# Routed experts by blocks of 128 slots in place of pairs of blocks, in an attention and mixture-of-experts kernel

## The chip, the core and the metric

The kernel runs on one core of a Trainium2 chip. A core has five engines that run their own instruction streams and meet only at semaphores: TensorE (PE), VectorE (DVE), ScalarE (ACT), GpSimd (POOL) and SyncE (SP). SP, ACT and POOL also issue DMA transfers between the chip's memory (HBM) and the on-chip memory. Matrix products land in PSUM, which has eight banks of 128 partitions by 512 fp32 values. The metric is the device time of one execution in microseconds, lower is better; what is shown before is the median of three timed runs and one profiled execution.

## What is computed

`x` has 4 sequences of 256 tokens with 256 channels. The first half of the kernel adds cross attention to it; the second half adds a feed-forward layer with two of eight routed experts per token and a shared expert. The part that matters here:

```python
    scores = xf @ gate_w.T                       # 1024 tokens, 8 experts
    ew, ei = jax.lax.top_k(scores, TOP_K)        # the two best
    ew = jax.nn.softmax(ew, axis=-1)
    x1 = jax.nn.silu(jnp.einsum('td,ehd->teh', xf, w_gate))
    x3 = jnp.einsum('td,ehd->teh', xf, w_up)
    expert_out = jnp.einsum('teh,edh->ted', x1 * x3, w_down)
    comb = jnp.einsum('ta,tae->te', ew, onehot)
    routed = jnp.einsum('te,ted->td', comb, expert_out)
    shared = jax.nn.silu(xf @ sh_gate.T) * (xf @ sh_up.T) @ sh_down.T
    sgate = jax.nn.sigmoid(xf @ se_gate_w.T)
    return (routed + sgate * shared).reshape(Bb, Tt, Cc)
```

`xf` is the layer norm of `x` behind the attention, and the whole is added to `x`. An expert has 128 hidden units, the shared one 256. Everything is fp32.

## The kernel before

**The routing by slots.** The kernel doesn't compute all experts for all tokens. Each token's normalised row, with its number and its lower expert's number behind it, is written twice to a list in HBM (`slots_dram`), in the region of each of its two experts: 16 indirect DMAs of GpSimd. The 2048 entries are then worked through in blocks of 128 rows, each of one expert. As each expert's last block may be part empty, there are at most 16 + 7 = 23 blocks (`BLOCKS`). VectorE works out a table with the first row (`row_of`) and the expert (`expert_of`) of each block. SP, PE and DVE each load what they need of it into registers (line 285, `TENSOR_LOAD`), since the addresses of row loads (SP), of down weights (PE) and of hidden weights (DVE) depend on it.

**One block.** SP loads its rows to `xg` (132 KB, six buffers, line 314). PE transposes them into PSUM (`gather_T`, line 1048), ACT copies the transpose to `xgT` (line 506). DVE copies the expert's gate and up weights to `hidden_w` (`stage`, line 798, four buffers). PE forms gate and up (`routed_hidden`, line 1064), ACT takes SiLU of the gate (`r_silu`, line 514), DVE multiplies by up (`r_act`, line 806), PE forms the down product (`routed_down`, line 1079), ACT copies it to `y_sb` (lines 522 and 526), and GpSimd scatters the 128 result rows to `routed_dram` (`send_y`, line 365) by places that DVE works out from the rows' tails (`places`, lines 776 and 780).

**By pairs.** Blocks go through this in pairs `p` of two (12 pairs, the last of one block). One PSUM bank holds the transposes of a pair, one its gate and up, one its two results. Each of `xgT`, `r_silu` and `r_act` has two buffers of a pair, `y_sb` has three (`NY`). All hand-overs are once a pair, except that from pair `SINGLE` = 9 on the results are copied and released block by block. PE's order in the loop is hidden(p), transposes of pair p + 2, down(p - 1). ACT's is SiLU(p), copy of the transposes of p + 2, copy of the results of p - 1. DVE's is `r_act`(p), weights of p + 2, places of p + 2. GpSimd only sends.

**Around the loop.** The order is written out by hand. The shared expert runs in two halves of 512 tokens and two units of 128 hidden values (`shared_gate`, `shared_up`, line 998; `shared_act`, line 759; `shared_down`, line 1034). Before the loop PE does gate(1,0), gate(1,1), up(1,0) and the first part of up(1,1); DVE does the residual of half 0 (`base(0)`, line 768), the product `shared_act(1, 0)`, the register load (`experts`), and weights and places of two pairs. The second part of up(1,1) and its product lie in the first turn of the loop. PE's first transposes wait for `shared_act(1, 0)`, as they take over its PSUM bank, and its first hidden products for both SiLUs of half 1. Behind the loop PE does `shared_down(1, ...)` and DVE `base(1)`. When all sends but the last have landed, SP and ACT load the lower half of the results (`lower_y`), and after the last the upper one (`upper_y`); DVE adds both with the tokens' shares (lines 811 and 817), and the output is stored.

## Time and profile before

| | before |
|---|---|
| three timed runs | 105.22, 107.85, 108.12 us, median 107.85 |
| profiled execution | 105.32 us, of which the span is 103.5 |
| PE busy | 85.5 us (83%) |
| DVE busy | 62.1 us (60%) |
| ACT busy | 46.5 us (45%) |
| POOL busy | 44.8 us (43%) |
| 23 sends of results | 23.6 us, mean 1025 ns |
| hidden products (line 1064) | 22.6 us, idle before them 1.1 |
| down products (line 1079) | 12.0 us, idle before them 0.3 |

The span is the time from the first to the last instruction of the profiled execution. Busy time counts the engines' own work, not semaphore waits or the issue of DMAs. Matmuls overlap in the array, so their durations can't be added up; a chain or the distance between starts tells what one costs. The trace puts every instruction at its time from the span's start; idle time before an instruction is given in brackets with what ended it.

### The profile page before, as it was taken

What the parts mean: (1) busy time and instruction counts of PE and PEld (TensorE: products, weight loads), DVE (VectorE), ACT (ScalarE), POOL (GpSimd) and SP (SyncE); (2) the same over time, 40 slices, a digit from 0 to 9 for tenths busy, and PEclk for the clock granted to TensorE, in tenths of its full rate; (3) what the DMA queues carried; (4) which work ended last, traced back from release to release, by engine and by line L of the source; (5) the groups of instructions that cost most, each with busy time, mean ns of one, the idle gap of its engine ahead of it and who ended that gap; (6) DMA issues with size and microseconds to landing.
All of it is one profiled execution on the core that took longest, in us unless ns stands there. A gap on an engine that the chain in (4) does not pass through costs nothing.

```text
span 103.5 us, 1864 instructions
## 1 busy us (share of the span) xinstructions
PE 85.5 (83%) x514; PEld 68.5 (66%) x514; DVE 62.1 (60%) x274; ACT 46.5 (45%) x104; POOL 44.8 (43%) x60
## 2 busy tenths in 40 slices
PE   6799999997999999996799999999999989600000
PEld 2386789895974478443789999999999968400000
DVE  1188989999999889202986444566444320604990
ACT  0556657758685991433036454466454361000000
POOL 7012002388676777300000567668667677710000
PEclk9999999999999999999999999999999999985555
DMA  2975999992232222256163434655412212059946
GB/s 20 376 267 133 410 413 401 333 348 77 93 108 104 104 104 104 104 142 177 26 186 104 112 107 134 188 152 161 154 46 100 96 56 101 0 90 355 369 180 225
DMA packets 10586, 17.50 MB, mean 169 GB/s; under 512 B 1613, under 2 KB 6095, under 8 KB 10576
## 3 DMA queue, kind: packets, MB, share of 16 engines
q1 hardware_dynamic: 7264, 10.63, 32.7%
q0 software_dynamic: 1872, 4.27, 11.2%
q10 hardware_dynamic: 1440, 2.49, 6.6%
q8 instruction: 4, 0.07, 0.3%
q14 instruction: 6, 0.05, 0.1%
HBM read 10.85 MB, written 7.44 MB: 177 GB/s over the span
## 4 chain that ended last, share of the span: by engine, by line
PE 64%; DMA 12%; DVE 12%; issue 3%; DVEq 3%; POOLq 1%; POOL 1%; ACT 1%; ACTq 0%
PE bank L1064 20%; PE bank L998 12%; PE bank L1079 9%; DMA upper_y<-routed_dram 6%; PE bank L1048 4%; DMA proj_sb<-proj 4%; PE bank L942 4%; PE bank L1034 4%; PE bank L898 3%; PE bank L923 3%; DVEq L285 2%; DMA routed_dram<-y_sb,place 2%; PE bank L906 2%; DVE x L642 2%; PE bank L907 2%
## 5 line engine op out<-in xcount | busy, mean ns | idle before, releaser
L365 POOL DMA_INDIRECT routed_dram<-y_sb,place x23 | 23.6, 1025 | 25.0 <-DVE place L780 15.4
L1064 PEld LDWEIGHTS bank<-xgT,hidden_w 128*128 128x128 f32 x184 | 22.4, 192 | 2.3 <-issue 1.8
L1064 PE MATMUL bank<-xgT,hidden_w 128*128 128x128 f32 x184 | 22.6, 275 | 1.1 <-DVE hidden_w L798 1.1
L352 POOL DMA_INDIRECT slots_dram<-rows,slot x16 | 15.7, 981 | 6.8 <-issue 4.4
L998 PE MATMUL bank<-xnT,ffn_sb 128*128 128x512 f32 (+1 forms) x36 | 14.6, 550 | 0.0
L806 DVE TENSOR_TENSOR r_act<-bank,r_silu 128x256 f32<-128x256 f32 (+1 forms) x12 | 5.0, 414 | 15.9 <-ACT r_silu L514 14.2
L1079 PE MATMUL bank<-ffn_sb,r_act 128*128 x46 | 12.0, 382 | 0.3 <-ACT y_sb L526 0.3
L514 ACT ACTIVATE r_silu<-bank 128x256 f32<-128x256 f32 (+1 forms) x12 | 4.5, 376 | 15.3 <-PE bank L1064 15.3
L998 PEld LDWEIGHTS bank<-xnT,ffn_sb 128*128 128x128 f32 x36 | 6.6, 190 | 5.5 <-issue 5.3
L798 DVE COPY hidden_w<-ffn_sb 128x512 f32 x23 | 8.7, 419 | 1.9 <-issue 1.9
L1079 PEld LDWEIGHTS bank<-ffn_sb,r_act 128*128 128x128 f32 x46 | 7.8, 190 | 1.2 <-issue 0.7
L506 ACT COPY xgT<-bank 128x512 f32<-128x512 f32 (+1 forms) x12 | 6.8, 568 | 3.5 <-PE bank L1048 3.0
L942 PE MATMUL bank<-mix,xT 128*128 128x276 f32 x32 | 8.2, 401 | 0.0
L1048 PE MATMUL bank<-ident,xg 128*128 128x128 f32 x46 | 7.1, 275 | 0.3 <-DMA xg<-slots_dram 0.3
L1034 PE MATMUL bank<-ffn_sb,sh_act 128*128 128x256 f32 x32 | 7.3, 382 | 0.0
L942 PEld LDWEIGHTS bank<-mix,xT 128*128 128x128 f32 x32 | 5.9, 190 | 1.3
L522 ACT COPY y_sb<-bank 128x512 f32<-128x512 f32 x9 | 5.3, 586 | 3.3 <-PE bank L1079 3.3
L1034 PEld LDWEIGHTS bank<-ffn_sb,sh_act 128*128 128x128 f32 x32 | 6.0, 190 | 1.0 <-DVE sh_act L759 0.2
L1048 PEld LDWEIGHTS bank<-ident,xg 128*128 128x128 f32 x46 | 5.3, 141 | 1.4 <-DVE sh_act L759 0.8
L768 DVE SCALAR_TENSOR_TENSOR x<-bank,sgate,x 128x256 f32<-128x256 f32 x8 | 3.5, 480 | 3.9 <-PE bank L1034 3.8
L811 DVE SCALAR_TENSOR_TENSOR x<-lower_y,share_lower,x 128x256 f32<-128x256 f32 x8 | 3.3, 478 | 4.2 <-DMA lower_y<-routed_dram 4.2
L344 POOL TENSOR_TENSOR rstd<-veps,neg_half 128x2 f32<-128x2 f32 x2 | 1.4, 715 | 9.1 <-DVE veps L607 9.1
(119 smaller groups left out, 128.9 us busy)
## 6 DMA issues: line engine op xcount, KB each, us to landing
ffn_sb<-ffn SPq DMA_DIRECT2D x2, 1536.0 KB, 9.6
xg<-slots_dram SPq DMA_DIRECT2D x23, 132.0 KB, 2.2
slots_dram<-empty SPq DMA_DIRECT2D x1, 1056.0 KB, 14.2
x_sb<-x ACTq DMA_DIRECT2D x4, 256.0 KB, 5.0
ffn_sb<-ffn SPq DMA_DIRECT2D x1, 768.0 KB, 4.3
lower_y<-routed_dram SPq DMA_DIRECT2D x2, 256.0 KB, 4.2
lower_y<-routed_dram ACTq DMA_DIRECT2D x2, 256.0 KB, 4.5
upper_y<-routed_dram SPq DMA_DIRECT2D x2, 256.0 KB, 5.6
```

The lines of the kernel that those rows point to most:

```text
L352: pool.indirect_dma_start(out=slots_dram[:, :], out_offset=bass.IndirectOffsetOnAxis(ap=slot[:, i, a:a + 1], axis=0), in_=rows[:, i, :], i ...
L365: pool.indirect_dma_start(out=routed_dram[0:planes * TOKENS, :], out_offset=bass.IndirectOffsetOnAxis(ap=place[:, j:j + 1], axis=0), in_=y ...
L506: act.copy(xgT[:, p % 2, :, 0:n, :], XG_BANK[p % 2][:, :].rearrange("p (k b n) -> p k b n", k=KT, b=2)[:, :, 0:n, :]).then_inc(xgT_stored, 1)
L522: act.copy(y_sb[:, p % NY, :, :], tiles(Y_BANK[p % 2])).then_inc(y_stored, 2)
L798: dve.tensor_copy(hidden_w[:, j % NW, :], ffn_sb[:, u, 0:2 * L].rearrange("p o n -> p (o n)")).then_inc(staged, 1)
L806: dve.tensor_tensor(r_act[:, p % 2, 0:n, :], hidden_of(p, 1), r_silu[:, p % 2, 0:n, :], ALU.mult).then_inc(r_act_ready, 1)
L942: last = pe.matmul(ps[:, 0:L + 2 * R], xT[:, b, k, t * P:(t + 1) * P], mix[:, b % 2, k, :], start=(k == 0), stop=(k == KT - 1))
L998: last = pe.matmul(ps[:, c0:c1], ffn_sb[:, E + u, c:c + P], xnT[:, k, h * N + c0:h * N + c1], start=(k == 0), stop=(k == KT - 1))
L1034: last = pe.matmul(tiles(SH_OUT[h][t // 2])[:, t % 2, :], sh_act[:, h, u, t * P:(t + 1) * P], ffn_sb[:, E + u, 2 * L:3 * L], start=(u == 0 ...
L1048: last = pe.transpose(ps[:, k, b, :], xg[:, j % NXG, k * P:(k + 1) * P], ident[:])
L1064: last = pe.matmul(hidden_of(p, kind)[:, j % 2, :], hidden_w[:, j % NW, c:c + P], xgT[:, p % 2, k, j % 2, :], start=(k == 0), stop=(k == K ...
L1079: last = pe.matmul(y_of(j), r_act[:, p % 2, j % 2, :], ffn_sb[:, u, 2 * L:3 * L].rearrange("p o n -> p (o n)"), start=True, stop=True)
```

## The change

The routed stage goes by blocks. PSUM banks, buffers and hand-overs are those of one block; a result has a buffer of its own among six, and is sent with a wait of its own. Gate and up, and the results, use other banks than before, so that the loop's first products wait for no bank of the shared expert. Places of a block are worked out in its own turn, and the weights three blocks ahead. VectorE loads its registers before `shared_act(1, 0)`, and TensorE forms up(1,0) before gate(1,1).

```diff
-PAIRS = (BLOCKS + 1) // 2
-JB = 2 * PAIRS
+JB = BLOCKS + 1
-NY = 3
+NY = 6
-        xgT = sb("xgT", [P, 2, KT, 2, P])
-        r_silu = sb("r_silu", [P, 2, 2, P])
-        r_act = sb("r_act", [P, 2, 2, P])
+        xgT = sb("xgT", [P, 2, KT, P])
+        r_silu = sb("r_silu", [P, 2, P])
+        r_act = sb("r_act", [P, 2, P])
-        y_sb = sb("y_sb", [P, NY, 2, L])
+        y_sb = sb("y_sb", [P, NY, L])
-        SH_OUT = [[bank[6], bank[3]], [bank[7], bank[2]]]
+        SH_OUT = [[bank[6], bank[3]], [bank[1], bank[3]]]
-        GU_BANK = [bank[1], bank[2]]
-        Y_BANK = [bank[6], bank[3]]
+        GU_BANK = [bank[4], bank[5]]
+        Y_BANK = [bank[6], bank[2]]
...
 SP, loads of rows
                 if j >= NXG:
-                    sp.wait_ge(xgT_ready, (j - NXG) // 2 + 1)
-                    sp.wait_ge(place_ready, (j - NXG) // 2 + 1)
+                    sp.wait_ge(xgT_ready, j - NXG + 1)
+                    sp.wait_ge(place_ready, j - NXG + 1)
...
 POOL, send_y
-                p, k = j // 2, j % 2
-                if p >= SINGLE:
-                    pool.wait_ge(y_stored, j + 1)
-                elif k == 0:
-                    pool.wait_ge(y_stored, 2 * p + 2)
-                if k == 0:
-                    pool.wait_ge(place_ready, p + 1)
+                pool.wait_ge(y_stored, j + 1)
+                pool.wait_ge(place_ready, j + 1)
...
 ACT
+            def store_xgT(j):
+                act.wait_ge(xgT_ready, j + 1)
+                if j >= 2:
+                    act.wait_ge(gu_ready, j - 1)
+                act.copy(xgT[:, j % 2], XG_BANK[j % 2][:, 0:KT * P].rearrange(
+                    "p (k n) -> p k n", k=KT)).then_inc(xgT_stored, 1)
...
+            def store_y(j):
+                act.wait_ge(y_ready, j + 1)
+                if j >= NY:
+                    act.wait_ge(y_sent[j % NY], 16 * (j // NY))
+                act.copy(y_sb[:, j % NY, :], y_of(j)).then_inc(y_stored, 1)
...
+            for j in range(BLOCKS):
+                routed_silu(j)
+                if j + 2 < BLOCKS:
+                    store_xgT(j + 2)
+                if j >= 1:
+                    store_y(j - 1)
+            store_y(BLOCKS - 1)
...
 DVE
+            def places(j):
+                dve.wait_ge(xg_in[j % NXG], 16 * (j // NXG + 1))
+                then(dve.tensor_scalar(plane[:, j:j + 1], xg[:, j % NXG, L + 1:L + 2], expert[:, j:j + 1],
+                                       float(TOKENS), ALU.is_equal, ALU.mult))
+                dve.tensor_tensor(place[:, j:j + 1], plane[:, j:j + 1], xg[:, j % NXG, L:L + 1].bitcast(I32),
+                                  ALU.add).then_inc(place_ready, 1)
...
+            def routed_act(j):
+                dve.wait_ge(r_silu_ready, j + 1)
+                if j >= 2:
+                    dve.wait_ge(y_ready, j - 1)
+                dve.tensor_tensor(r_act[:, j % 2, :], hidden_of(j, 1), r_silu[:, j % 2, :],
                                   ALU.mult).then_inc(r_act_ready, 1)
...
             base(0)
-            shared_act(1, 0)
             experts()
             stage(0)
-            places(0)
             stage(1)
-            places(1)
+            shared_act(1, 0)
+            stage(2)
             routed_shares()
-            for p in range(PAIRS):
-                routed_act(p)
-                if p + 2 < PAIRS:
-                    stage(p + 2)
-                    places(p + 2)
-                if p == 0:
+            for j in range(BLOCKS):
+                routed_act(j)
+                if j + 3 < BLOCKS:
+                    stage(j + 3)
+                if j == 0:
                     shared_act(1, 1)
+                places(j)
...
 PE
+            def routed_hidden(j):
+                if j >= 2:
+                    pe.wait_ge(r_act_ready, j - 1)
+                pe.wait_ge(xgT_stored, j + 1)
+                pe.wait_ge(staged, j + 1)
...
+            def routed_down(j):
+                if j < 2:
+                    pe.wait_ge(base_ready, 1)
                 else:
+                    pe.wait_ge(y_stored, j - 1)
+                pe.wait_ge(r_act_ready, j + 1)
...
             shared_gate(1, 0)
+            shared_up(1, 0)
             shared_gate(1, 1)
-            shared_up(1, 0)
...
+            for j in range(BLOCKS):
+                routed_hidden(j)
+                if j + 2 < BLOCKS:
+                    gather_T(j + 2)
+                if j == 0:
                     shared_up(1, 1, [1])
                 else:
+                    routed_down(j - 1)
+            routed_down(BLOCKS - 1)
```

VectorE's order between the residual of half 0 and its first `r_act`, before (`L285` is the register load, the `ISA` rows set an address from a register, `L759` is the shared product):

```order
L768 SCALAR_TENSOR_TENSOR x<-bank,sgate,x 128x256 x4
L759 TENSOR_TENSOR sh_act<-bank,sh_silu 128x512
L285 TENSOR_LOAD expert_of
L798 ISA
L798 COPY hidden_w<-ffn_sb 128x512
L798 ISA
L798 COPY hidden_w<-ffn_sb 128x512
```

and with the change (its line numbers are 27 to 33 lower there: `L741`, `L732`, `L271`, `L766`):

```order
L741 SCALAR_TENSOR_TENSOR x<-bank,sgate,x 128x256 x4
L271 TENSOR_LOAD expert_of
L766 ISA
L766 COPY hidden_w<-ffn_sb 128x512
L766 ISA
L766 COPY hidden_w<-ffn_sb 128x512
L732 TENSOR_TENSOR sh_act<-bank,sh_silu 128x512
L766 ISA
L766 COPY hidden_w<-ffn_sb 128x512
```

The load and two copies of weights now stand ahead of the shared product, a third behind it, and no places are worked out here.

TensorE's order at the loop's entry, before (`L998` is shared gate or up, `L1048` transposes of rows, `L1064` hidden products, `L1079` a down product with its address):

```order
L998 MATMUL bank<-xnT,ffn_sb 128x512
L1048 MATMUL bank<-ident,xg 128x128 x8
L1064 MATMUL bank<-xgT,hidden_w 128x128 x8
L1048 MATMUL bank<-ident,xg 128x128 x4
L998 MATMUL bank<-xnT,ffn_sb 128x512
L1064 MATMUL bank<-xgT,hidden_w 128x128 x8
L1048 MATMUL bank<-ident,xg 128x128 x4
L1079 ISA
L1079 MATMUL bank<-ffn_sb,r_act 128x256
L1079 ISA
L1079 MATMUL bank<-ffn_sb,r_act 128x256
```

and with the change:

```order
L964 MATMUL bank<-xnT,ffn_sb 128x512
L1011 MATMUL bank<-ident,xg 128x128 x4
L1024 MATMUL bank<-xgT,hidden_w 128x128 x4
L1011 MATMUL bank<-ident,xg 128x128 x2
L964 MATMUL bank<-xnT,ffn_sb 128x512
L1024 MATMUL bank<-xgT,hidden_w 128x128 x4
L1011 MATMUL bank<-ident,xg 128x128 x2
L1035 ISA
L1035 MATMUL bank<-ffn_sb,r_act 128x256
L1024 MATMUL bank<-xgT,hidden_w 128x128 x4
L1011 MATMUL bank<-ident,xg 128x128 x2
```

Two blocks are transposed ahead of the first hidden product in place of four, and each step is half as long; the number of matmuls is the same.

## Rows read from the trace of the kernel before

**Rows 1.** Busy time by stretch: PE, PEld, DVE, ACT, POOL, then clock.
```profile
49.85:86.13 36.28, 35.99 (x271) 33.98 (x272) 18.59 (x84) 16.81 (x35) 19.68 (x20) 1.00 0.38 116
```

**Rows 2.** Chain of waits at the loop's entry: start, duration, what.
```profile
46.42 0.05 issue
46.47 2.32 DVEq L285
...
49.85 2.02 PE bank L1064 x16
```

**Rows 3.** Order of time ahead of the loop, all engines: start, duration, idle before.
```profile
40.18 1.81 DVE L768 SCALAR_TENSOR_TENSOR x<-bank,sgate,x 128x256 f32<-128x256 f32 x4
...
40.91 6.17 PE L998 MATMUL bank<-xnT,ffn_sb 128*128 128x512 f32 x14
...
46.33 0.69 DVE L759 TENSOR_TENSOR sh_act<-bank,sh_silu 128x512 f32<-128x512 f32 x1 [4.34 <-PE bank L998]
...
47.08 0.87 PE L1048 MATMUL bank<-ident,xg 128*128 128x128 f32 x6
...
48.28 0.44 PE L1048 MATMUL bank<-ident,xg 128*128 128x128 f32 x2 [0.33 <-DMA xg<-slots_dram]
```

**Rows 4.** Order of time on ACT, single shapes near the loop's end.
```profile
79.96 0.37 ACT L506 COPY xgT<-bank 128x256 f32<-128x256 f32 x1
...
82.55 0.38 ACT L514 ACTIVATE r_silu<-bank 128x256 f32<-128x256 f32 x1 [1.12 <-PE bank L1064]
...
84.31 0.28 ACT L514 ACTIVATE r_silu<-bank 128x128 f32<-128x128 f32 x1 [0.52 <-PE bank L1064]
```

**Rows 5.** Order of time on DVE, single shapes near the loop's end.
```profile
80.44 0.42 DVE L798 COPY hidden_w<-ffn_sb 128x512 f32 x1
80.77 0.21 DVE L776 TENSOR_SCALAR plane<-xg,expert 128x1 f32<-128x1 f32 x1
81.01 0.16 DVE L780 TENSOR_TENSOR place<-plane,xg 128x1 int32<-128x1 f32 x1
...
84.62 0.29 DVE L806 TENSOR_TENSOR r_act<-bank,r_silu 128x128 f32<-128x128 f32 x1 [1.23 <-ACT r_silu L514]
```

**Rows 6.** Chain of waits, one pair of the steady loop.
```profile
59.34 1.78 PE bank L1064 x16
61.12 0.44 PE bank L1048 x4
61.56 0.87 PE bank L1079 x4
```

**Rows 7.** Chain of waits at the loop's exit.
```profile
84.27 0.45 PE bank L1079 x2
...
85.18 0.24 issue
85.42 0.71 PE bank L1079 x2
...
86.21 0.38 ACT y_sb L526
...
89.94 2.12 DMA routed_dram<-y_sb,place
```

**Rows 8.** Loads of rows (line 314): time from issue to landing.
```profile
DMA to landing us min/median/max: 1.9/2.2/3.4
```

**Rows 9.** Order of time on ACT and POOL: a copy of results, and sends.
```profile
80.84 0.59 ACT L522 COPY y_sb<-bank 128x512 f32<-128x512 f32 x1 [0.51 <-PE bank L1079]
...
60.79 0.98 POOL L365 DMA_INDIRECT routed_dram<-y_sb,place  x1 [0.68 <-issue]
...
80.62 1.09 POOL L365 DMA_INDIRECT routed_dram<-y_sb,place  x1 [0.30 <-issue]
82.20 0.98 POOL L365 DMA_INDIRECT routed_dram<-y_sb,place  x1 [0.48 <-issue]
```

**Rows 10.** Order of time on DVE behind the loop: the first adds of results.
```profile
94.66 3.26 DVE L811 SCALAR_TENSOR_TENSOR x<-lower_y,share_lower,x 128x256 f32<-128x256 f32 x8 [4.18 <-DMA lower_y<-routed_dram]
```

More of the change, by code:

```diff
@@ L263, in wait_for_lower @@
             for i in range(NY):
-                mine = [j for j in range(LAST) if j // 2 % NY == i]
+                mine = [j for j in range(LAST) if j % NY == i]
                 queue.wait_ge(y_sent[i], 16 * len(mine))
         def wait_for_upper(queue):
-            queue.wait_ge(y_sent[LAST // 2 % NY], 16 * rows_sent(LAST // 2 % NY))
+            queue.wait_ge(y_sent[LAST % NY], 16 * rows_sent(LAST % NY))
         def load_lower(queue, k):
@@ L770, in base @@
                 last.then_inc(base_ready, 1)
-            def places(p):
-                for j in range(2 * p, 2 * p + blocks_in(p)):
-                    dve.wait_ge(xg_in[j % NXG], 16 * (j // NXG + 1))
-                    last = dve.tensor_scalar(plane[:, j:j + 1], xg[:, j % NXG, L + 1:L + 2], expert[:, j:j + 1],
-                                             float(TOKENS), ALU.is_equal, ALU.mult)
-                then(last)
-                for j in range(2 * p, 2 * p + blocks_in(p)):
-                    last = dve.tensor_tensor(place[:, j:j + 1], plane[:, j:j + 1],
-                                             xg[:, j % NXG, L:L + 1].bitcast(I32), ALU.add)
-                last.then_inc(place_ready, 1)
+            def places(j):
[4 more added lines that the diff above has]
+                                  ALU.add).then_inc(place_ready, 1)
             on_chip = []
```

137 lines of the change are left out of this document (32 added, 105 removed).

## The prediction

> **What bounds the kernel now.** I read three views in turn: busy time by stretch, the chain of waits, the order of time on each engine. In the routed stage TensorE does 35.99 us of work in 36.28 us at granted clock 1.00 [rows 1]: while the stage runs, it is the bound. VectorE (18.59), ScalarE (16.81) and GpSimd (19.68) each have about half their time over, so what they gain or lose in total is worth nothing; only when they hand something over counts.
>
> The chain of waits shows two places where TensorE isn't the bound. The first is the entry. VectorE takes the shared product at 46.33, then its register load of 2.32 us, and only then copies the first weights; TensorE's first hidden product starts at 49.85 [rows 2]. VectorE had stood idle for 4.34 us before that product, since its part of the residual ended at 40.18 + 1.81 = 41.99 [rows 3]. TensorE, done with shared work at 47.08, transposed four blocks and then waited [rows 3]. The second place is the exit. TensorE's last down product ends at 86.13 and its copy at 86.59, but the last send starts at 89.94 and lands 2.12 us later [rows 7]. Since results are released by pairs, GpSimd starts late: the first pair is copied long after its first block was done, and the last seven sends, from 82.20 [rows 9] to 89.94, follow each other at 7.74/6 = 1.29 us, a queue that TensorE has left behind.
>
> **Entry.** The register load moves into the idle stretch: 41.99 + 2.32 = 44.3, and two weight copies at 0.42 [rows 5] end by 45.3 with their issue. The second shared up product now comes before the second gate product. From 40.91 eight passes at 6.17/14 = 0.44 us give gate and up of unit 0 [rows 3], so up ends at 44.4 where it ended at about 46.2; the shared product (0.69, [rows 3]) runs 45.3 to 46.0 and is there before TensorE wants its buffers at 47.08. The second gate product, 1.7 us later, feeds a SiLU that ScalarE fits into its own idle time, and whose product is wanted only inside the loop. So at 47.08 TensorE starts as before, but transposes two blocks ahead in place of four. One block takes 0.44 alone [rows 3], its copy 0.37 [rows 4], with about 0.2 for two hand-overs: hidden product 0 starts at 48.1, not 49.85: **minus 1.75 us**. Ends of the unknown: nothing won, if the loads of rows are late (blocks 0 to 2 were there by then, since their transposes ran through, and only the fourth was waited for, 0.33 us [rows 3]); or 1.9 if the hand-overs overlap.
>
> **Steady loop.** Per pair TensorE spends 1.78 + 0.44 + 0.87 = 3.09 us with no gap between [rows 6]; per block the same instructions take 1.54. They are not more, only interleaved finer. What changes is the notice that each wait gets. Say hidden product j ends at t. SiLU of one block takes 0.28 [rows 4], the product 0.29 [rows 5], hand-overs 0.1: r_act is ready at t + 0.7. TensorE comes to down product j after 0.22 + 0.43 + 0.89 + 0.22 = 1.76 us: 1.06 us to spare (it was 2.6). ScalarE per block: 0.28 + 0.37 + 0.37 = 1.02 [rows 4] of 1.54. VectorE: 0.29 + 0.42 + 0.21 + 0.16 = 1.08 [rows 5]. All fit, so I cost the split at zero for both; their cover is TensorE, and without it the extra would be one fixed part per instruction, 2 x 1.02 against 0.38 [rows 4] + 0.59 + 0.59 [rows 9] = 1.56 per pair on ScalarE, 0.48 us. The transposes of two more blocks now lie inside the loop: 2 x 0.22 = **plus 0.44 us**. The load of row block j + 6 now waits for the places of block j, which follow its r_act: issued at t + 1.6, landed after 2.2, at most 3.4 us [rows 8], so at t + 5.0 at worst; TensorE wants it at four periods, t + 6.2. The cover is 1.2 us; the load was issued a pair and more earlier before. TensorE's waits double (one set per block). I bound that by nothing and by 0.05 us a block, 1.1 us in all, which is the size of the bare step behind a wait in the chain [rows 2]; I take 0, since all of them are satisfied in advance and its rows stand gapless across pair boundaries.
>
> **Exit.** Call H the end of the last hidden product: it was 84.27, with down product 21 ending 0.45 later [rows 7]. Now H = 84.27 - 1.75 + 0.44 = 82.96. Down product 21 ends at 83.41, its copy at 83.86. A send starts 0.77 us after its copy: the copy that ends at 80.84 + 0.59 = 81.43 has its send at 82.20 [rows 9]. Send 21 starts at 84.63. Send 20 came 1.3 us before, as the period without a transpose is 1.32, so there is no queue. Down product 22 no longer waits for a copy, only for r_act 22 (H + 0.65, then 0.24 to start, 0.71 to run [rows 7]): it ends at 84.55, and its send could start at 85.8; 1.29 after send 21 it does, at 85.92. Before, 89.94: **minus 4.0 us**. Of this the last 2.7 are the queue that is gone, the rest is the entry less the two transposes.
> Behind the last send nothing changes: the lower half of the results is loaded when send 21 has landed, the upper when send 22 has, the adds begin at 94.66 after 4.18 us of waiting for the load [rows 10]. The residual of the second half ended before that wait, at 90.5; it moves ahead with TensorE by about 1.6, to 88.9, and the load's landing by 4.0, to 90.7, so it stays hidden. Two more semaphores are waited for at the queues, under 0.1.
>
> **Sum.** The profiled execution took 105.32 us (span 103.5): minus 4.0 gives 101.3 (span 99.5). The three timed runs read 105.22, 107.85 and 108.12, so two of four executions are 2.6 us above the others, and the one trace shows nothing of why. Their mean with the profiled one is 106.6; minus 4.0 is 102.6, which I forecast, between 101.3 and 103.9 for the two groups.
>
> **Rivals.**
> *A. GpSimd's turn per send becomes the bound (slower).* Before, every second send of a pair had no wait of its own and started 0.30 after its predecessor; now each waits for its own copy. If the 0.77 us between copy and send can't overlap the send before, a turn is 0.99 to 1.11 plus 0.77, about 1.83. The first send starts at 52.9 (down product 0 ends at 51.7: 48.1 + 0.89 + 0.22 + 0.86 + 0.89 + 0.22 + 0.43, and 1.2 for copy and send), the last at 52.9 + 22 x 1.83 = 93.2, 3.2 after today's: 108.5 on the profiled execution's scale, 109.8 on the forecast's. It decides from a turn of (89.94 - 52.9)/22 = 1.68 on. For it: the idle before the first send of a pair, 0.68 [rows 9]. Against: the copy that ended at 81.43 did so while a send ran until 81.71, and the next started at 82.20, 0.49 after it, not 0.77 [rows 9]. With 0.49 a turn is 1.48 to 1.60 and would cost at most 22 x 0.06 = 1.3, less as soon as a queue forms and the gap falls to 0.30.
>
> *B. VectorE's weight copies hold up the sends.* A second send of a pair, which runs beside such copies, took 1.09, a first one without them 0.98 [rows 9]. Before, two copies lay together and touched every second send; now one lies under each. At the measured 0.11 a turn is 1.40, still under 1.54, and the sum stands. If instead each send had to stand through a whole copy, a turn were 0.98 + 0.42 + 0.30 = 1.70: last send at 52.9 + 22 x 1.70 = 90.3, no gain, 107.0 on the forecast's scale. The Trainium skill (SBUF — State Buffer, the section "SBUF: two separate sides") says that an fp32 copy within SBUF on VectorE takes the port that GpSimd needs to write descriptors, and that the later one blocks fully. By that rule this rival would be the case, and the sum would be near zero; the trace's 0.11 speaks against its full size.
>
> *C. Finer grain leaves gaps on TensorE.* 0.05 to 0.1 us at each of 21 blocks, by hand-overs or by a late load of rows: 1.1 to 2.1 back, so 103.7 to 104.7. The Trainium skill (VectorE: DVE Perf Modes, the section on the TRN2 errata) advises tiles of 512 elements and more, because every instruction pays its fixed part anew; SiLU of 256 in 0.38 against 0.28 for 128 agrees, but the engines that pay it have a third of their time free.
>
> *D. The entry wins nothing*, as the hidden product waits for rows or for ScalarE's copy and not for weights: 4.0 - 1.75 = 2.25 is left, 104.4.
>
> **Chances.** Forecast 0.55, A 0.06, B 0.07, C 0.20, D 0.07, and 0.05 for things I haven't seen on either side. A measurement of this kernel can tell about 2% (2.2 us) from no change. Faster by more than that are the forecast, half of C, D in part: 0.72; within it B, the rest of C and D: 0.21; slower A: 0.07. The range goes from 100.9 (forecast on the lower group, with the hand-overs overlapped) to 105.8 (C's far end, 104.7, with the 1.3 of the upper group nearly whole); outside are A, B and a part of the rest.
>
> **What would show it.** Right: hidden product 0 at about 48.1 with VectorE's register load at about 42; TensorE gapless from there at 1.54 a block; first send near 53, sends at 1.54 with 0.4 to 0.5 idle between, the last at about 86, and everything after at the old distances. Wrong: idle of TensorE ahead of down or hidden products that grows with the block number (C), sends at 1.6 and more apart with copies waiting (A, B), or a first hidden product still near 49.5 (D). If VectorE's r_act starts later than 0.4 us behind the hidden product, my account of its load is at fault.

## The result, and the profile after

The changed kernel takes 101.94 us (median of four runs, 101.56 to 104.01); the kernel before, beside it on the same chip, 106.55 us (105.22 to 108.12). The ratio is 0.9677, with a 95% interval of 0.9612 to 0.9741; like all ratios here it is formed from the faster group of executions on each side (101.56, 101.58 and 102.30 against 105.22 and 105.25), so it is nearer to 1 than the quotient of the medians. The profiled execution took 101.56 us (span 99.8) where that of before took 105.32 (103.5): 3.76 us less, where I had predicted 4.0. The forecast of 102.6 us was 0.7 us too high.

The entry first. The order of time on VectorE (start, duration in us; in brackets the idle before it and what ended it):

```profile
40.68 1.41 DVE L741 SCALAR_TENSOR_TENSOR x<-bank,sgate,x 128x256 f32<-128x256 f32 x3
44.21 0.76 DVE L766 COPY hidden_w<-ffn_sb 128x512 f32 x2 [2.12 <-issue]
44.89 0.68 DVE L732 TENSOR_TENSOR sh_act<-bank,sh_silu 128x512 f32<-128x512 f32 x1
```

The register load, 2.73 us from 41.33 by the view of its line, ends at 44.06 and is what fills the 2.12 us of "issue" ahead of 44.21. It lies where VectorE had little else to do, and the shared product follows it. TensorE, same view:

```profile
47.02 0.60 PE L1011 MATMUL bank<-ident,xg 128*128 128x128 f32 x4
47.87 1.16 PE L1024 MATMUL bank<-xgT,hidden_w 128*128 128x128 f32 x8 [0.24 <-ACT xgT L486]
```

TensorE comes to its transposes at 47.02 (47.08 before) and has its first hidden product at 47.87 in place of 49.85 [rows 2, 3]. It no longer waits for weights: what ends its wait is ScalarE's copy of the transposed rows.

One block of the steady loop on TensorE, ScalarE and VectorE:

```profile
60.74 1.05 PE L1024 MATMUL bank<-xgT,hidden_w 128*128 128x128 f32 x8
61.63 0.38 PE L1011 MATMUL bank<-ident,xg 128*128 128x128 f32 x2
61.84 0.28 ACT L493 ACTIVATE r_silu<-bank 128x128 f32<-128x128 f32 x1 [0.52 <-PE bank L1024]
61.85 0.60 PE L1035 MATMUL bank<-ffn_sb,r_act 128*128 x2
...
62.15 0.29 DVE L773 TENSOR_TENSOR r_act<-bank,r_silu 128x128 f32<-128x128 f32 x1 [0.60 <-ACT r_silu L493]
62.29 1.05 PE L1024 MATMUL bank<-xgT,hidden_w 128*128 128x128 f32 x8
```

From 60.74 to 62.29 is 1.55 us, and busy time by stretch shows that TensorE has no gap in any block (PE, PEld, DVE, ACT, POOL, then the clock):

```profile
53.00:83.00 30.00, 30.00 (x235) 29.00 (x235) 17.33 (x78) 18.52 (x58) 19.40 (x20) 1.00 0.46 141
```

TensorE is busy for all of 30.00 us. It answers to [rows 1], where 0.29 of 36.28 us were idle. ScalarE does more than before in less time (18.52 of 30.00 us, against 16.81 of 36.28), the fixed part of its many more instructions (58 in 30.00 us, against 35 in 36.28).

GpSimd's sends: two of the loop, and the last four.

```profile
59.00 0.98 POOL L346 DMA_INDIRECT routed_dram<-y_sb,place  x1 [0.56 <-DVE place L750]
60.55 0.98 POOL L346 DMA_INDIRECT routed_dram<-y_sb,place  x1 [0.56 <-DVE place L750]
...
82.15 0.98 POOL L346 DMA_INDIRECT routed_dram<-y_sb,place  x1 [0.56 <-issue]
83.48 0.98 POOL L346 DMA_INDIRECT routed_dram<-y_sb,place  x1 [0.34 <-issue]
84.80 0.98 POOL L346 DMA_INDIRECT routed_dram<-y_sb,place  x1 [0.34 <-issue]
86.09 0.98 POOL L346 DMA_INDIRECT routed_dram<-y_sb,place  x1 [0.31 <-issue]
```

They keep TensorE's period of 1.54 us with 0.56 us of it idle. The releaser that the rows name, `place`, is that of the next block and misleads: the send at 60.55 follows the copy of its own result, which ends at 59.77, by 0.78. Hardly any queue forms: the last two results are copied at 84.03 and 85.18, 1.15 apart, and their sends start 1.29 apart, so the last send waits for its turn 0.14 us longer than for its result. It starts at 86.09 in place of 89.94 [rows 7].

Behind the loop, on VectorE:

```profile
88.27 0.88 DVE L741 SCALAR_TENSOR_TENSOR x<-bank,sgate,x 128x256 f32<-128x256 f32 x2 [0.78 <-PE bank L1000]
90.86 3.25 DVE L778 SCALAR_TENSOR_TENSOR x<-lower_y,share_lower,x 128x256 f32<-128x256 f32 x8 [1.72 <-DMA lower_y<-routed_dram]
94.04 3.25 DVE L784 SCALAR_TENSOR_TENSOR x<-upper_y,share_upper,x 128x256 f32<-128x256 f32 x8
```

The wait for the lower load shrank from 4.18 us [rows 10] to 1.72: the adds moved by 3.80 us (94.66 to 90.86), the residual ahead of them by less. Both groups of adds run back to back, so the upper load is never waited for. The chain of waits reads alike, after:

```profile
84.80 2.11 DMA routed_dram<-y_sb,place
87.11 3.66 DMA lower_y<-routed_dram
90.86 2.84 DVE x L778 x7
```

and before, behind the landing of the last send [rows 7]:

```profile
92.47 6.36 DMA upper_y<-routed_dram
```

The end now hangs on the landing of send 21, which releases the lower load. Before, it hung on send 22 and the upper load.

### The profile page after: what moved, and what is told of

Its sections match the earlier page's. It is cut to its first block, busy times and chain, and to the rows that moved or that the text cites. A ratio compares the mean times of both kernels' runs of the same rounds, so it can differ in the third digit from the quotient of the medians.

```text
span 99.8 us, 1992 instructions
## 1 busy us (share of the span) xinstructions
PE 85.6 (86%) x514; PEld 68.9 (69%) x514; DVE 64.7 (65%) x285; ACT 50.3 (50%) x135; POOL 43.8 (44%) x60
## 4 chain that ended last, share of the span: by engine, by line
PE 36%; issue 17%; POOL 17%; DVE 15%; DMA 10%; ACT 1%; DVEq 1%; POOLq 0%; SPq 0%
POOL routed_dram L346 17%; PE bank L964 13%; PE bank L908 4%; DMA proj_sb<-proj 4%; PE bank L1000 4%; DMA lower_y<-routed_dram 4%; PE bank L864 3%; DVE x L778 3%; PE bank L889 3%; DVE x L784 3%; PE bank L872 2%; DMA routed_dram<-y_sb,place 2%; PE bank L1024 2%; DVE x L615 2%; PE bank L873 2%
## 5 line engine op out<-in xcount | busy, mean ns | idle before, releaser
L346 POOL DMA_INDIRECT routed_dram<-y_sb,place x23 | 22.6, 984 | 22.0 <-DVE place L750 20.5
L1024 PEld LDWEIGHTS bank<-xgT,hidden_w 128*128 128x128 f32 x184 | 24.1, 191 | 2.0 <-ACT xgT L486 0.5
L1024 PE MATMUL bank<-xgT,hidden_w 128*128 128x128 f32 x184 | 24.3, 275 | 0.2 <-ACT xgT L486 0.2
L773 DVE TENSOR_TENSOR r_act<-bank,r_silu 128x128 f32<-128x128 f32 x23 | 6.7, 291 | 16.0 <-ACT r_silu L493 15.9
L1035 PE MATMUL bank<-ffn_sb,r_act 128*128 x46 | 13.8, 383 | 0.5 <-ACT y_sb L499 0.5
L493 ACT ACTIVATE r_silu<-bank 128x128 f32<-128x128 f32 x23 | 6.4, 278 | 13.2 <-PE bank L1024 13.2
L766 DVE COPY hidden_w<-ffn_sb 128x512 f32 x23 | 9.5, 417 | 2.1 <-issue 2.1
L499 ACT COPY y_sb<-bank 128x256 f32<-128x256 f32 x23 | 8.6, 373 | 2.3 <-PE bank L1035 1.1
L486 ACT COPY xgT<-bank 128x256 f32<-128x256 f32 x23 | 8.5, 373 | 0.6 <-PE bank L1011 0.5
L1011 PE MATMUL bank<-ident,xg 128*128 128x128 f32 x46 | 8.6, 273 | 0.0
L741 DVE SCALAR_TENSOR_TENSOR x<-bank,sgate,x 128x256 f32<-128x256 f32 x8 | 3.5, 479 | 3.4 <-PE bank L1000 3.3
L456 ACT ACTIVATE rows<-x,shift,rstd 128x256 f32<-128x256 f32 x8 | 4.4, 594 | 1.8 <-DVE shift L640 1.8
```

Of the source, the lines that this page charges most:

```text
L346: pool.indirect_dma_start(out=routed_dram[0:planes * TOKENS, :], out_offset=bass.IndirectOffsetOnAxis(ap=place[:, j:j + 1], axis=0), in_=y ...
L486: act.copy(xgT[:, j % 2], XG_BANK[j % 2][:, 0:KT * P].rearrange("p (k n) -> p k n", k=KT)).then_inc(xgT_stored, 1)
L499: act.copy(y_sb[:, j % NY, :], y_of(j)).then_inc(y_stored, 1)
L766: dve.tensor_copy(hidden_w[:, j % NW, :], ffn_sb[:, u, 0:2 * L].rearrange("p o n -> p (o n)")).then_inc(staged, 1)
L773: dve.tensor_tensor(r_act[:, j % 2, :], hidden_of(j, 1), r_silu[:, j % 2, :], ALU.mult).then_inc(r_act_ready, 1)
L1011: last = pe.transpose(XG_BANK[j % 2][:, k * P:(k + 1) * P], xg[:, j % NXG, k * P:(k + 1) * P], ident[:])
```

## The experiments

The experiments ran on several chips. Each ratio is against the kernel before on the same chip, run beside the experiment. The kernel before took 105.68 us (median) beside the first four, 109.65 beside the next two, 109.14 beside the four after these, and 105.88 beside the last two.

**The entry alone**, put into the kernel before, whose loop stays in pairs:

```
             base(0)
-            shared_act(1, 0)
             experts()
             stage(0)
-            places(0)
             stage(1)
+            shared_act(1, 0)
+            places(0)
             places(1)
...
-            shared_gate(1, 1)
             shared_up(1, 0)
+            shared_gate(1, 1)
```

> The kernel before, by pairs, with only the entry changed: VectorE loads its registers and copies four blocks' weights ahead of the shared product, and TensorE forms up(1,0) before gate(1,1). If the entry was held by VectorE's late weights, the first hidden product starts as soon as TensorE has transposed four blocks (the fourth landed at 48.25 and its transposes took 0.44) : at about 48.7 instead of 49.85, and all behind it moves by 1.1 us, the queue of sends with it: span 102.4 against 103.5, ratio 0.99. If the entry was worth the whole 1.98 us that the change shows there, 101.5. If it was held by something else, no change.

Measured: 104.92 us, ratio 0.9939 (0.9904 to 0.9974). TensorE in the order of time:

```profile
47.66 0.86 PE L1048 MATMUL bank<-ident,xg 128*128 128x128 f32 x4
48.76 0.97 PE L1048 MATMUL bank<-ident,xg 128*128 128x128 f32 x4 [0.25 <-DMA xg<-slots_dram]
49.57 1.95 PE L1064 MATMUL bank<-xgT,hidden_w 128*128 128x128 f32 x16
```

From TensorE's arrival to its first hidden product it is 1.91 us, before 2.77: 0.86 won, where I expected 1.1. Four blocks must still be transposed there, and the rows of the later two come late. The entry therefore is worth 0.86 us by itself and nearly 2 only together with the loop by blocks.

**The loop alone**, with the entry of before:

```
             base(0)
+            shared_act(1, 0)
             experts()
             stage(0)
             stage(1)
-            shared_act(1, 0)
             stage(2)
...
-            shared_up(1, 0)
             shared_gate(1, 1)
+            shared_up(1, 0)
```

> The changed kernel with the entry of before: the shared product first, then the register load, and gate(1,1) before up(1,0). The work by blocks and the sends by blocks stay. The first hidden product then waits for one copy of weights behind the load: about 49.4 to 49.5, 1.6 us later than in the changed kernel and 0.4 before the kernel before. The steady loop and the exit are those of the changed kernel, so span 101.4. If the gain came from the entry alone, 103; if from the blocks alone, 100.

Measured: 105.46 us, four runs from 103.16 to 106.25; the runs scatter too much for a ratio. The fastest has the span that was expected (101.4); the profiled one (105.44) shows a term that my sums lack. TensorE in the order of time, then busy time by stretch with the clock behind the counts:

```profile
47.47 0.66 PE L1011 MATMUL bank<-ident,xg 128*128 128x128 f32 x4
49.88 1.86 PE L1024 MATMUL bank<-xgT,hidden_w 128*128 128x128 f32 x8 [1.75 <-DVE hidden_w L766]
```

```profile
50.00:53.00 3.00, 3.00 (x12) 2.48 (x13) 1.68 (x9) 0.65 (x2) 0.00 (x0) 0.51 0.01 3
53.00:56.00 3.00, 3.00 (x22) 2.51 (x21) 1.88 (x7) 0.96 (x3) 0.00 (x0) 0.92 0.00 0
```

From its arrival at 47.47 to the first hidden product it is 2.41 us, 0.36 less than before (2.77), as expected. TensorE idles for 1.75 us of it for the weights, and right behind that its granted clock is 0.51, the lower of its two levels (1.2 GHz). The same eight hidden passes take 1.86 us, in the change 1.16. From first hidden product to last send it is 39.85 us here and 38.22 in the change: 1.6 us that the loop's arithmetic has no term for. It comes in some executions only: the mean clock of the whole run was 0.939 here and 0.940 in a second run, but 0.958 and 0.961 in the other two, the fastest among them. The last sends are again 1.28 to 1.33 us apart, so the entry has no part in that.

**Copies of results singly**, in the kernel before, with its steps still in pairs (the last three pairs already did so):

```
-        SINGLE = PAIRS - 3
+        SINGLE = 0
...
-                    if j > 2 * SINGLE:
+                    if j >= 2:
                         pe.wait_ge(y_stored, j - 1)
...
```

> The kernel before, by pairs, but every pair's results are copied and released to GpSimd block by block, as before only in the last three pairs (the first down product also waits for the second shared product). If it is the release by pairs that makes GpSimd late, most of the queue of 2.7 us at the exit goes, and the span is near 101. If it is the order of the work by pairs (both results of a pair come at the end of its 3.09 us, and three blocks' results come after the last hidden product), the sends of the last seven blocks start only 0.6 to 0.9 us earlier: span 102.8, ratio 0.99 to 1.0.

Measured: 106.28 us, ratio 0.9949 (0.9885 to 1.0013). The last send starts at 89.67 in a profile whose routed stage starts 0.33 later than that of before, 0.6 earlier against TensorE. GpSimd at the end:

```profile
80.28 1.03 POOL L365 DMA_INDIRECT routed_dram<-y_sb,place  x1 [0.30 <-issue]
...
84.51 0.98 POOL L365 DMA_INDIRECT routed_dram<-y_sb,place  x1 [0.38 <-ACT y_sb L526]
...
89.67 0.99 POOL L365 DMA_INDIRECT routed_dram<-y_sb,place  x1 [0.30 <-issue]
```

Copying block by block isn't enough. Down products j and j + 1 still follow each other 0.43 us apart and a send's turn takes 1.29, so a pair's second result waits behind the first one's send, and the end queue stays. What removes it is TensorE's order, which brings one result per period.

**Up product late**, the change with only this edit taken back:

```
-            shared_up(1, 0)
             shared_gate(1, 1)
+            shared_up(1, 0)
```

> The changed kernel with up(1,0) back behind gate(1,1); VectorE's register load stays ahead of the shared product. TensorE has the same work before its first transposes. The shared product then runs from about 46.3 to 47.0, just before TensorE gets to its transposes at 47.0. If the register load is the whole of the entry's gain, the span stays 99.8 (0 to 0.1 more). If the moved up product has a part in it, VectorE is late with the product and the first hidden product slips by up to 0.7 us.

Measured: 102.1 us, ratio 0.9663 (0.9618 to 0.9709). TensorE arrives at 47.36 and has its first hidden product at 48.26, 0.90 later; in the change 0.85. This edit is worth nothing that can be seen; of the entry's two edits it is the register load that gains.

**Four buffers of rows** in place of six (`NXG = 6` to `4`):

> The changed kernel with four buffers of rows in place of six. In its trace the places of block j are ready 2.35 us after hidden product j starts; a load takes some 0.3 to issue and 2.2 to land, so rows of block j + 4 are there 4.8 us after that start, while TensorE wants them at 3.98. If my account of the cover of the row loads is right (1.2 us at the worst landing with six buffers, none with four), a block takes about 1.82 us instead of 1.54 and the span grows by 4 to 5 us. If the loads are further ahead than I think, it stays at 99.8.

Measured: 112.9 us beside 109.65 of before, ratio 1.0337 (1.018 to 1.0494), with 4.5 us of TensorE's waits for rows in seven pieces. In the order of time:

```profile
58.22 1.05 PE L1024 MATMUL bank<-xgT,hidden_w 128*128 128x128 f32 x8
...
63.26 0.41 PE L1011 MATMUL bank<-ident,xg 128*128 128x128 f32 x2 [0.91 <-DMA xg<-slots_dram]
...
64.03 0.72 PE L1024 MATMUL bank<-xgT,hidden_w 128*128 128x128 f32 x5
```

These three blocks take 5.81 us, 1.94 each in place of 1.54 (1.82 was expected); over the whole loop it is 1.90, part of which belongs to the chip, as the run of the change below will show. So the loads' cover is less than two periods (3.1 us): with two buffers less it is gone. That fits the 1.2 us of the prediction and doesn't measure it.

**Second half's up product behind the loop**, so that the loop starts without it:

```
-                if j == 0:
-                    shared_act(1, 1)
                 places(j)
+            shared_act(1, 1)
...
-            shared_up(1, 1, [0])
...
             routed_down(BLOCKS - 1)
+            shared_up(1, 1)
```

> The changed kernel with the last shared up product (both parts, 1.72 us of TensorE) and its product on VectorE moved behind the routed loop, ahead of the shared down product. TensorE then reaches its transposes at 46.2 and waits for the first rows until about 46.4; the loop is 0.86 shorter: the last hidden product and with it sends 21 and 22 come 1.5 us earlier. If the chain over the sends alone sets the end, the span falls to 98.3. If the residual of half 1 takes its place, it ends near 90.1 (loop's end at 83.1, 1.72 up, 1.0 for the product, 3.46 down, 0.9 residual) while the load lands at 89.4, and the gain is only 0.7: span 99.1.

Measured: 108.26 us beside 109.65 of before on this chip, ratio 0.9836 (0.9759 to 0.9913). VectorE in the order of time:

```profile
95.41 0.88 DVE L741 SCALAR_TENSOR_TENSOR x<-bank,sgate,x 128x256 f32<-128x256 f32 x2 [0.78 <-PE bank L999]
96.32 3.25 DVE L778 SCALAR_TENSOR_TENSOR x<-lower_y,share_lower,x 128x256 f32<-128x256 f32 x8
```

The adds now start as the residual ends, without a wait for the load: the work moved behind the loop has used up the 1.72 us of slack and become the bound itself. A span of 99.1 was expected and the profile has 105.2, but the loop has gaps on this chip, and the change itself did not run there; whether this version gains anything over it is not shown.

**The change once more, on another chip:**

> The changed kernel itself, on the same chip and beside the same runs of the kernel before as the next three, since chips differ by some per cent. Expected: ratio 0.968 as before.

Measured: 108.11 us beside 109.14, ratio 0.9894 (0.9805 to 0.9983). This misses what I expected. The profiled execution (111.98 us, the slowest of the six, so good only for where such time can go; some of its time was lost earlier, with the granted clock at 0.50 between 32 and 34 us) is gapless from 55 to 75 us and then is not:

```profile
75.00:80.00 5.00, 4.08 (x33) 3.74 (x32) 1.56 (x7) 1.30 (x5) 3.08 (x4) 1.00 0.59 162
80.00:85.00 5.00, 4.22 (x32) 4.07 (x33) 2.65 (x12) 2.52 (x9) 2.85 (x3) 1.00 0.42 130
```

```profile
76.27 1.05 PE L1024 MATMUL bank<-xgT,hidden_w 128*128 128x128 f32 x8
...
79.92 0.28 ACT L493 ACTIVATE r_silu<-bank 128x128 f32<-128x128 f32 x1 [2.30 <-PE bank L1024]
80.23 0.29 DVE L773 TENSOR_TENSOR r_act<-bank,r_silu 128x128 f32<-128x128 f32 x1 [2.73 <-ACT r_silu L493]
80.78 0.69 PE L1035 MATMUL bank<-ffn_sb,r_act 128*128 x2 [1.69 <-ACT y_sb L499]
```

TensorE stands still for 1.69 us in the middle of the loop, while VectorE and ScalarE, too, do less (1.56 and 1.30 us of 5 from 75 to 80, against 3.14 and 3.13 in the 5 before), at granted clock 1.00. The rows show who is first. The hidden product at 76.27 is done by 77.32, ScalarE's last copy by 77.63, but its SiLU of that product starts at 79.92, after 2.30 us of idle time. `r_act` follows, ends at 80.52, and the down product that reads it starts 0.26 later. So a standstill of ScalarE, less the cover of about 1 us, becomes TensorE's idle time. The traces of the next two runs on this chip have it too: a SiLU behind 2.32 us of idle time, then 0.93 of TensorE, and one behind 1.81, then 0.42. Nothing in the traces explains why ScalarE's stream stops.

**Down products of the last half by unit**, on top of the version with the up product behind the loop, so that the first unit's can run while the second unit's product is made:

```
-            shared_down(1, 0)
-            shared_down(1, 1)
+            for u in range(SH):
+                pe.wait_ge(sh_act_ready, SH + u + 1)
+                for t in range(2 * LT):
+                    last = pe.matmul(OUT1[t], sh_act[:, 1, u, t * P:(t + 1) * P],
+                                     ffn_sb[:, E + u, 2 * L:3 * L], start=(u == 0), stop=(u == SH - 1))
...
```

> The changed kernel with the last shared up product and its product on VectorE behind the routed loop, as in e6_up_behind, and in addition the shared down product of half 1 by units: first the four matmuls of unit 0, which need nothing of the moved product, then those of unit 1, each result in a bank of its own. If the residual of half 1 was what held e6_up_behind, the wait for VectorE's product (about 1.0 us) is now covered by 1.73 us of matmuls and the end moves with the sends: 1.5 us less than the changed kernel, 98.3 where that has 99.8, ratio to the kernel before about 0.953. If the sends came late in e6_up_behind for another reason (its rows and sends waited on the chip it ran on), the gain over the changed kernel is under 0.7.

Measured: 107.5 us, ratio 0.9779 (0.9655 to 0.9902), beside 108.11 and 0.9894 of the change on the same chip. It is the fastest version on that chip by point, but the two intervals overlap, so that it beats the change is not shown; the 0.953 that I expected is missed. The residual ends at 96.94 and the adds start at 96.97: still the residual bounds them, but the lower load is no longer early. The transfer issued at 93.25 took 3.51 us and landed at 96.77, so this edit has used up what there was to gain at this place.

**The idle stretch filled.** The loop alone once more, with eight products of zeros put into its wait for weights:

```
             gather_T(1)
+            for _ in range(8):
+                pe.matmul(bank[5][:, :], warm[:], warm[:].rearrange("p (o n) -> p o n", o=1).broadcast_to(
+                    [P, N // P, P]), start=True, stop=True)
```

> e2_blocks_only (the entry of before, the rest of the change) with eight matmuls of a zero tile, 512 columns each (about 1.8 us at full clock, their result is never read), in the stretch in which TensorE waits for the first weights. In e2_blocks_only that stretch was 1.75 us idle and the granted clock then stood at 0.51 between 50 and 53. If the idle stretch is what lowers the clock, it stays at 1.00 here, the first eight hidden matmuls take 0.9 to 1.2 us in place of 1.86, and most runs come at 103.2, as the one undisturbed run of e2_blocks_only did, with the first hidden product no later. If the clock falls for another reason, the first stretch is as slow as there (105.4).

Measured: 109.61 us, ratio 1.0078 (1.0024 to 1.0131), on the chip where the change itself has 0.9894. TensorE, and the stretch behind:

```profile
50.26 1.89 PE L1092 MATMUL bank<-warm 128*128 128x512 bf16 x8
52.17 1.13 PE L1024 MATMUL bank<-xgT,hidden_w 128*128 128x128 f32 x8
```

```profile
53.00:56.00 3.00, 3.00 (x22) 2.47 (x21) 2.40 (x10) 1.22 (x5) 0.00 (x0) 1.00 0.00 0
```

The eight hidden passes take 1.13 us, not 1.86, and the clock stays at 1.00. In all ten runs its mean was 0.949 or more, where two of four runs of the loop alone had 0.939 and 0.940. So the slow start goes with the idle stretch ahead of it, as far as ten runs against four on another chip can show. The total says nothing on it, since TensorE stood idle for 0.97 of the 33.83 us from 52.17 and for 1.32 of the next 6, in standstills like those of the change on this chip. It does say that the loop by blocks without the better entry gains nothing there.

**Weight copies moved under the start of the sends**: the copy is made ahead of r_act and not behind it.

```
-                if j >= NW:
-                    dve.wait_ge(gu_ready, j - NW + 1)
+                if j >= NW - 1:
+                    dve.wait_ge(gu_ready, j - NW + 2)
...
-                routed_act(j)
                 if j + 3 < BLOCKS:
                     stage(j + 3)
+                routed_act(j)
```

> The changed kernel with each weight copy of VectorE ahead of r_act in place of behind it, so that it runs from about 0.05 to 0.47 us behind each hidden product's end and a send, which starts at 0.34, begins while the copy runs. In the changed kernel the copy begins 0.26 us after the send and a send takes 0.98. If a running copy holds up a send that begins under it, sends take 1.09 as every second one did before; if only their overlap in general counted, the changed kernel's would have been long already, so 0.98 here too would leave the 1.09 open. The time moves by no more than 0.1 either way: r_act comes 0.1 later and has 1 us to spare, and a turn of 1.40 still fits in 1.54.

Measured: 110.19 and 108.11 us, two runs, too few for a ratio. Sends on GpSimd, and copies on VectorE, in the order of time:

```profile
57.92 1.12 POOL L346 DMA_INDIRECT routed_dram<-y_sb,place  x1 [0.41 <-issue]
59.45 1.14 POOL L346 DMA_INDIRECT routed_dram<-y_sb,place  x1 [0.40 <-issue]
60.99 1.24 POOL L346 DMA_INDIRECT routed_dram<-y_sb,place  x1 [0.41 <-issue]
62.54 0.98 POOL L346 DMA_INDIRECT routed_dram<-y_sb,place  x1 [0.31 <-issue]
...
67.17 0.98 POOL L346 DMA_INDIRECT routed_dram<-y_sb,place  x1 [0.31 <-issue]
...
80.80 1.05 POOL L346 DMA_INDIRECT routed_dram<-y_sb,place  x1 [1.16 <-issue]
```

```profile
57.76 0.43 DVE L766 COPY hidden_w<-ffn_sb 128x512 f32 x1 [0.60 <-PE bank L1024]
59.30 0.43 DVE L766 COPY hidden_w<-ffn_sb 128x512 f32 x1 [0.60 <-issue]
60.94 0.43 DVE L766 COPY hidden_w<-ffn_sb 128x512 f32 x1 [0.70 <-PE bank L1024]
...
80.57 0.43 DVE L766 COPY hidden_w<-ffn_sb 128x512 f32 x1 [0.63 <-PE bank L1024]
```

A send that starts while a copy runs is longer: 1.24 us with 0.38 of the copy left (60.99 against 60.94 + 0.43), 1.14 with 0.28 left, 1.12 with 0.27, 1.05 with 0.20. One that starts clear of copies takes 0.98 (67.17). The surplus is the rest of the copy less some 0.12, which also gives the 1.09 of the kernel before (0.23 left); I had expected 1.09 here too, but more of the copy is left. The send at 62.54 breaks the rule with 0.98. It starts 0.02 behind the start of a copy, which takes 0.47 in place of 0.43; here the send seems to have come first. In the change the copy comes 0.26 us after the send's start (60.81 against 60.55), and all 23 sends take 0.98 to 1.00. A copy later inside a send is less harmless: in the run with copies of results singly one starts 0.49 into the second sends of pairs, and those take 1.03.

**The kernel before against itself, and the change, on one more chip:**

> The kernel before itself, unchanged, with a profile. Question: does the kernel before hide stalls of ScalarE's, VectorE's and SyncE's instruction streams (its r_act is 2.6 us ahead of the down product) which the change does not (1.06 us)? Ratio to before 1.00. Theory (hiccups are hidden before, shown after): in the span 50 to 86 us of this profile TensorE is idle under 0.3 us although ScalarE and VectorE show idle times put down to issue or to an unknown queue of over 1 us. Rival (the chip costs both kernels the same, elsewhere): TensorE's idle time in the steady loop is as large here as in the change on the same chip, or none in both.

> The change itself, unchanged, beside the kernel before on the same chip. If the chip's TIME before is 105 to 106 us (as on the first chip): ratio 0.965 to 0.97 and a steady loop of 1.54 us per block without a gap. If it is 108 us or more (as on the chip of the second run of the change): by the theory that finer grain lets stalls through, ratio 0.98 to 1.00 and over 1 us of TensorE idle in the steady loop, more than in the kernel before of the same call; by the rival, that the miss of 0.989 came from other causes than the loop, ratio 0.965 to 0.975.

Measured: the kernel before against itself 0.9999 (0.9962 to 1.0036), which is how far such a comparison can be trusted. The change: 102.03 us beside 105.88, ratio 0.964 (0.959 to 0.9691), and busy time in the loop:

```profile
50.00:84.00 34.00, 33.94 (x261) 32.22 (x260) 19.88 (x88) 20.24 (x64) 19.88 (x21) 1.00 0.43 127
```

This was a chip on which the kernel before takes 106 us, and the first result comes back, by the branch that both theories share for such a chip. So whether the kernel before hides the standstills that the change shows stays undecided: its profile here (35.71 of 36.00 us busy) holds none to hide.

## Why the prediction was right, step by step

**The bounds.** Right. TensorE in the loop, VectorE's load at the entry and the queue of sends at the exit were the three places that mattered.

**Entry.** Predicted minus 1.75, measured minus 1.98 (49.85 to 47.87), of which 0.06 is the earlier arrival. I gave one block's transposes, its copy and the hand-overs 1.0 us; the trace has 0.85. What I said of the up product was not needed: with its move taken back it is 0.90. The gain isn't that of the register load alone: from TensorE's arrival on, the early load by itself gives 0.86, the loop by blocks by itself 0.36 (2.77 to 2.41), and both together 1.92 (2.77 to 0.85). With the load early, four blocks' transposes and late rows are what is left in the way; with the blocks alone, the weights are.

**Steady loop.** Zero was predicted and measured. By my account r_act is ready 0.7 us behind the hidden product and TensorE asks for it after 1.76. In the trace the next instruction follows the hidden product at 61.63, r_act ends at 62.15 + 0.29 = 62.44 and the down product starts at 63.40: 0.81 and 1.77, a cover of 0.96 where I had 1.06. The product itself ends at 60.74 + 1.05 = 61.79, and counted from there `r_act` starts 0.36 and is ready 0.65 us later, which is what I had; the last sign of the prediction, 0.4, is only just kept. That the loads of rows have a cover of less than two periods was confirmed by taking two buffers away; its 1.2 us was not measured.

**The miscounted term.** H, the end of the last hidden product, was to move by minus 1.31 (minus 1.75 plus 0.44). In the order of time the down products behind it start at 84.11 before and at 83.02 now: minus 1.09. By the entry as measured it would be minus 1.54. The 0.45 between is one down product (0.43): I read the one behind H in [rows 7] as number 21, but it is 20. In the order by pairs, blocks 20 and 21 both come behind H, so 20 down products stand ahead of it, and with the change 21. The better entry (0.23) hid half of that error. Sends 21 and 22 start at 84.80 and 86.09, predicted 84.63 and 85.92: both 0.17 late.

**Exit.** Minus 4.0 predicted, minus 3.85 measured at both last sends, and minus 3.76 on the whole. Of the 3.85 the earlier end of the loop gives 1.09 and the queue 2.76, where I had 1.3 and 2.7. That an even stream of results removes the queue stands. The reason that I gave for the queue, "since results are released by pairs", does not: released one by one in all pairs, the last send came only 0.6 us earlier and the queue stayed. It is the order of TensorE's work, two results at the end of each 3.09 us and three behind the last hidden product, that makes it. The change alters both, so the forecast didn't depend on which it was. What stands behind the last send I had wrong in one respect that cost nothing: the chain now goes over send 21's landing and 6.5 us of adds, so the upper load, and with it send 22, has slack.

**The rivals.** A is false: the send at 84.80 starts 0.77 after its copy (84.03) but only 0.34 after the send before it ended (84.46). The 0.77 overlaps the send before, turns go down to 1.29, and a turn of 1.68 is never needed. B at full size is false in the change; its 0.11 exists, but needs a copy that is running as a send starts, and by blocks there is none. The Trainium skill (SBUF — State Buffer, the section "SBUF: two separate sides") has the later of the two blocked fully. The trace agrees for the start of a send (the surplus grows with what is left of the copy) and disagrees for the rest of it: a copy that starts 0.26 us into a send takes its usual 0.42 and adds nothing. C did not happen on the chips where the kernel before takes 105 to 106 us. On the one where it takes 109 the gain is 1%. One trace there shows the way, a standstill of ScalarE of 2.30 us against a cover of 1; that such standstills make up the whole of the missing gain, and that the kernel before hides them, is argued and not shown. They aren't the even gap per block that rival C names. D is false: the hidden product starts at 47.87. In A, the terms of down product 0's end add up to 51.6, not 51.7, which changes nothing.

**The levels.** I put the median between two groups, 101.3 and 103.9, and predicted 102.6. The median came out at 101.94 and in the repeat at 102.03, near the lower group: of these eight executions one lies in the upper group (104.01), where it had been two of four. That I carried the split over had no reason in the trace. This and the 0.24 us of the sum make up the forecast's miss, in opposite directions. That the median is off by only 0.7 is in part luck. The lower end of the range, 100.9, is also 0.25 below what its own terms give (101.3 less 0.15).

The runs hint at why the split doesn't carry over. The mean granted clock of the whole run is 0.940 or less in 18 of 58 executions of the kernel before and in 3 of 8 of the two versions that keep its entry, the loop alone and the copies singly. It is so in none of the 53 executions of all other versions, in which TensorE doesn't stand idle for its first weights. So the wait that the change takes away may bring a lower clock in some executions, a gain that no sum here has. No trace of such an execution of the kernel before was kept, so this isn't shown.

## What to carry over

When a queue outlives the engine that feeds it, look at how evenly results arrive there: an even stream at the bound's own period removes the queue, and copying earlier without changing the producer's order does not. Put a fixed-time step such as a register load into the idle stretch of its engine before anything that is waited for, and count after such a move which instructions stand ahead of the point you measure from and which behind. Finer steps cost the slack of each hand-over; where an engine stands still for longer than this slack, as ScalarE did on one chip, the bound engine waits too, so measure on more than one chip.

## What the runs showed of the hardware

- In one trace an idle stretch of 1.75 us on TensorE was followed by a granted clock of 0.51 over the next 3 us and 0.92 over the 3 after that: some 1.6 us more than the idle time itself. With the stretch filled by eight products of zeros the clock read 1.00 and the first passes took 1.13 in place of 1.86 us. So a short wait in front of a dense loop can cost twice its length. It doesn't always: two of the four runs with that wait kept a mean clock of 0.958 and 0.961, and in the trace of the kernel before the clock is 1.00 behind 1.13 us of idle time.
- An indirect DMA's 0.98 us on GpSimd grows by up to 0.26 when a VectorE copy within SBUF is under way as it starts, by the rest of that copy less 0.12. It isn't touched by one that starts 0.26 later (0.98 to 1.00 in 23 sends); one that starts 0.49 later went with 1.03.
- On one chip ScalarE's stream stood still for 2.30 us with its input ready, and TensorE lost 1.69 us by it. On the chips where the kernel before takes 105.7 to 106.6 us neither trace of the change has such a gap.
- Chips differ: the kernel before takes 105.7 to 106.6 us (medians) on three and 109.1 to 109.7 on two, and the same change is worth 3.2 to 3.6% on the former and 1.1% (0.2 to 2.0%) on one of the latter.
